# An adaLN block on one core: the setup phase dissolved into the first steps of the pipeline

## The chip, the cores and the metric

One core of a Trainium2 chip. The time is device microseconds of one execution, given as the median of several runs; lower is better. The profile is one further execution, recorded by the hardware profiler.

## The reference, cut to what matters

```python
x = L0_attn_x                                    # 8 batches, 512 tokens, 128 features, f32
mod = (_silu(L0_c) @ L0_wmod).reshape(8, 6, 1, -1)
sa, ca, ga, sb, cb, gb = (mod[:, i] for i in range(6))
ga = (2 * (ga >= 0) - 1) * jnp.maximum(jnp.abs(ga), 0.25)   # gb the same
h = _layernorm(x) * (1 + ca) + sa
x = x + ga * linear_attention(h)                 # 16 heads of 8, causal, elu features, projection, layer norm
h = _layernorm(x) * (1 + cb) + sb
x = x + gb * ffn(h)                              # layer norm, softmax attention, layer norm, mixture of 8 experts
```

Everything that depends on the conditioning vector c (the six rows of `mod` for each batch) is a small computation: SiLU of an 8 x 128 tensor, one product with 128 x 768 weights, signs and maxima of the gates.

## The kernel before

The kernel is three blocks in a row, each with its own instruction streams for the five engines, and a barrier of all engines between them: `setup_phase`, `attention` and `route` (the experts).

**Setup.** SP issues all loads on its one DMA queue (lines 208 to 215): c, the constants, the modulation weights, all of x in four loads of 512 KB, then the weights, those of the linear attention in twelve small loads (four of q and k, four bias columns, four of v). ACT computes the exponential of SiLU (L232), DVE the rest (L266 to L270), PE turns it (L241) and multiplies it with the modulation weights (L244 for shift and scale of the first norm, L247 for the other four rows). DVE works out the gates (L283 to L302), puts weights into another order of columns (L297, L305, L309), and copies the turned weights out (L317, L318). POOL fills the constant parts of the tiles `values` and `k_stack` (L225, L227). SP writes the modulation rows to memory, where they are read back broadcast to all partitions.

**Attention.** A software pipeline written out by hand: steps s from -3 to 8, each with eight slots d. In step s the engines work on stage a of batches s+3, s+2 and s+1, stage b (the causal linear attention, eight units g = 8s + d, one a slot) of batch s, and stage c of batches behind. Each engine has a list of `if d == ...` with what it does in a slot.
- Stage a: DVE takes statistics of x (`a_stats`, L1210 to L1217), POOL the reciprocal root (`a_rstd`, L643 to L647), ACT normalises (L1393), PE turns (`a_turn`, L877), ACT applies scale and shift of c (`a_h_out`, L1399), PE projects (`a_query` L882, `a_key` L887, `a_value` L892), ACT and DVE make features (exp L1404, ReLU L1234, sum L1239) and split them into three bf16 parts (ACT L1409, L1413; DVE L1245; POOL L651), which SP stores (L362, `linear_parts`).
- SP then reads the parts back in another arrangement into `q_stack` and `k_stack`, twelve loads (L380; for batch 0 in two halves of twelve). The stacks of two batches are kept in turn. PE multiplies them in `products` (L815), one unit ahead of the numerators: the first one of batch 1 stands in the last slot of step 0.
- DVE adds the output bias in `output` (L1206), the first of which waits for the seventeen late loads (L350), issued by SP at the start of the block: biases, gate and projection weights, gains, and `mod4` and `gb_all`, the broadcast modulation rows (2 MB and 512 KB). Before the first step, POOL clears the two tiles `spad` (L743); PE waits for both and DVE waits for both too.

## Time and profile before

| | us |
|---|---|
| median of 3 runs | 821.37 |
| lowest, highest | 821.14, 822.47 |
| the profiled execution's own time | 819.17 |
| its span | 817.4 |
| mean granted TensorE clock | 0.921 |
| PE busy | 656.6 (80%) |
| DVE busy | 601.7 (74%) |
| ACT busy | 495.7 (61%) |
| POOL busy | 435.2 (53%) |
| HBM read, written | 43.20 MB, 21.45 MB |

The span is the time from the first to the last recorded instruction; the execution's own time has 1.8 us more around it. Busy shares are means over phases that have different limits. The granted clock is TensorE's, as a share of its upper level of 2.4 GHz; 0.50 is the lower level, 1.2 GHz. Loads are recorded where they are issued (SPq); the transfer comes behind that.

### The profile page before, as it was taken

The page shows a single profiled execution, that of the slowest core. Times are in us where ns is not written, and L with a number is a line of the kernel's source. Part 1 is how long each engine was busy: PE and PEld are TensorE (multiplying, and loading weights), DVE is VectorE, ACT ScalarE, POOL GpSimd, SP SyncE. Part 2 cuts the span into 40 slices and gives each one's busy share as a digit, 9 for nine tenths or more (in the row PEclk, how much of TensorE's full clock was granted, in tenths as well). Part 3 has the DMA queues.
Part 4 walks back from the last instruction along what each step waited for, and adds up shares of the span by engine and source line. Part 5 has one row for each costly group of instructions (what it writes and reads, how often), then busy time and mean ns, then how long its engine had stood idle before and what let it go on. Part 6 is the DMA issues. An engine that isn't in the chain of part 4 may idle for free. (4 is left out here: it accounts for less than half of the span.)

```text
span 817.4 us, 16278 instructions
## 1 busy us (share of the span) xinstructions
PE 656.6 (80%) x5448; PEld 342.0 (42%) x5448; DVE 601.7 (74%) x1439; ACT 495.7 (61%) x1009; POOL 435.2 (53%) x953
## 2 busy tenths in 40 slices
PE   1338978899887797899999999999999734668784
PEld 0225656666655312223323333332332323567774
DVE  3445799998977998799999999999996154222332
ACT  0251456666545358788888888888888613233342
POOL 4220164765565433126666666666766734666653
PEclk9967999999999869999999999999999955988988
DMA  6334222533353211047212111121200012323210
GB/s 167 137 102 131 83 75 78 155 104 96 113 171 103 78 39 40 3 115 218 78 39 73 47 59 60 51 68 38 81 21 20 20 48 70 105 75 89 78 55 14
DMA packets 39409, 65.37 MB, mean 80 GB/s; under 512 B 6460, under 2 KB 32127, under 8 KB 36320
## 3 DMA queue, kind: packets, MB, share of 16 engines
q1 hardware_dynamic: 35584, 54.57, 21.8%
q0 software_dynamic: 3744, 9.77, 4.2%
q8 instruction: 45, 0.74, 0.4%
q14 instruction: 36, 0.29, 0.1%
HBM read 43.20 MB, written 21.45 MB: 79 GB/s over the span
## 5 line engine op out<-in xcount | busy, mean ns | idle before, releaser
L1457 ACT ACTIVATE arena<-pair 128x512 f32<-128x512 f32 x512 | 281.5, 602 | 51.7 <-PE pair L959 49.9
L1262 DVE TENSOR_REDUCE arena<-bank 128x1 f32<-128x512 f32 x388 | 250.6, 684 | 9.3 <-PE bank L938 8.4
L959 PE MATMUL pair<-q_stack,k_stack 49*128 49x512 bf16 x512 | 161.7, 387 | 8.0 <-ACT arena L1457 6.6
L938 PE MATMUL bank<-k_stack,q_stack 48*128 48x512 bf16 x388 | 137.5, 395 | 11.3 <-DVE arena L1262 4.8
L970 PE MATMUL bank<-arena,values 128*9 128x512 f32 x1024 | 135.6, 602 | 0.2 <-ACT arena L1457 0.2
L1181 DVE TENSOR_TENSOR arena<-bank,cst 128x512 f32<-128x512 f32 x128 | 82.2, 684 | 28.4 <-PE bank L815 27.9
L708 POOL TENSOR_TENSOR arena<-arena 128x1 f32<-128x1 f32 (+6 forms) x364 | 80.3, 221 | 28.5
L1262 DVE TENSOR_REDUCE arena<-pair 128x1 f32<-128x512 f32 x124 | 84.5, 681 | 1.7 <-PE pair L938 1.6
L938 PEld LDWEIGHTS bank<-k_stack,q_stack 48*128 48x128 bf16 x388 | 33.3, 93 | 110.6 <-issue 27.6
L959 PEld LDWEIGHTS pair<-q_stack,k_stack 49*128 49x128 bf16 x512 | 42.4, 93 | 60.1 <-ACT arena L1457 37.7
L1789 ACT ACTIVATE fq_all<-bank 128x512 f32<-128x512 f32 x39 | 23.2, 594 | 72.9 <-remote 37.8
L1377 ACT ACTIVATE arena<-bank,den_eps 128x512 f32<-128x512 f32 x32 | 21.7, 678 | 52.9 <-PE bank L841 52.9
L1869 PE MATMUL pair<-arena,fq_all 128*128 x208 | 32.7, 308 | 22.1 <-issue 12.5
L938 PE MATMUL pair<-k_stack,q_stack 48*128 48x512 bf16 x124 | 49.1, 396 | 1.2 <-DVE arena L1292 1.0
L1820 POOL DMA_INDIRECT out_dram<-arena,e_token_u x32 | 32.3, 1010 | 29.6 <-DVE arena L1697 22.8
L1860 PE MATMUL bank<-arena,h_all 128*128 128x128 f32 x312 | 47.8, 303 | 0.1
L1860 PEld LDWEIGHTS bank<-arena,h_all 128*128 128x128 f32 x312 | 44.8, 221 | 0.0
L830 PE MATMUL bank<-fq_all,arena 128*128 128x128 f32 x192 | 32.2, 292 | 14.0 <-ACT arena L1377 13.7
L656 POOL TENSOR_SCALAR arena<-arena 128x4 f32<-128x4 f32 x24 | 5.5, 229 | 70.7 <-DVE arena L1217 70.5
L1688 DVE TENSOR_SCALAR arena<-pair,lnw 128x128 f32<-128x128 f32 x39 | 15.9, 408 | 36.5 <-PE pair L1853 23.7
L841 PE MATMUL bank<-arena,values 128*9 128x128 f32 x1024 | 42.4, 286 | 0.0
L815 PE MATMUL bank<-q_stack,k_stack 48*128 48x128 bf16 x512 | 26.7, 227 | 17.9 <-DMA k_stack<-linear_parts 11.8
(261 smaller groups left out, 1269.5 us busy)
## 6 DMA issues: line engine op xcount, KB each, us to landing
linear_parts<-arena SPq DMA_DIRECT2D x8, 768.0 KB, 3.7
softmax_parts<-arena SPq DMA_DIRECT2D x8, 768.0 KB, 6.4
token_rows<-arena SPq DMA_DIRECT2D x32, 192.0 KB, 1.9
arena<-in_L_ffn_w_dram SPq DMA_DIRECT2D x16, 256.0 KB, 5.2
q_stack<-softmax_parts SPq DMA_DIRECT2D x16, 192.0 KB
k_stack<-softmax_parts SPq DMA_DIRECT2D x16, 192.0 KB
q_stack<-linear_parts SPq DMA_DIRECT2D x14, 192.0 KB
k_stack<-linear_parts SPq DMA_DIRECT2D x14, 192.0 KB
```

What stands on the lines that cost most here:

```text
L708: done(pool.tensor_tensor(half[:, 0:w], src[:, 0:w], src[:, w:2 * w], ALU.add))
L830: pe.matmul(b_nm[:, cols], spad[u][:, c - 1, cols], k.fq_all[:, b * L + c * P:b * L + (c + 1) * P], start=(gg == 0), stop=False, skip_grou ...
L841: last = pe.matmul(b_nm[VW * j:VW * j + E + 1, cols], vp[u][:, c, GH * (2 * hp + gg) + j, :], b_am[:, g % 2, gg, j, :], start=(c == 0), st ...
L938: pe.matmul(bank[:], qs[b % 2][rows, slot, qt * P:(qt + 1) * P], ks[b % 2][rows, slot, :], start=True, stop=True).then_inc(d_s_m, 1)
L959: pe.matmul(b_s[s % len(b_s)][:], ks[u][rows, 2 * g + x, kt * P:(kt + 1) * P], qs[u][rows, 2 * g + x, :], start=True, stop=True).then_inc( ...
L970: last = pe.matmul(b_num[VW * q:VW * q + E + 1, :], vp[b % 2][:, kt, GH * g + q, :], pt[:, kt % 2, q % 2, q // 2, :], start=(kt == 0), sto ...
L1181: dve.tensor_tensor(b_am[:, g % 2, gg], k.tiles(b_at[gg][:], GH), k.rep(k.causal, GH), ALU.mult).then_inc(s_am, 1)
L1262: dve.reduce_max(mx[:, m % 2, col:col + 1], bank[:], AX).then_inc(d_s_mr, 1)
L1457: act.activation(pt[:, kt % 2, x, half, :], b_s[s % len(b_s)][:], ACT.Exp, scale=SCALE).then_inc(d_s_e, 1)
L1820: pool.indirect_dma_start(out_rows, rows_at(token_u, j), yo[j], None, bounds_check=T * P - 1, oob_is_err=False).then_inc(s_sc, 16)
L1860: last = pe.matmul(b_up[j % R3][:, c * P:(c + 1) * P], w1c[j % R4][:, c * P:(c + 1) * P], xt[j % R4], start=True, stop=True)
L1869: last = pe.matmul(b_dn[j % R3][:, 0:D], hid[j % R4][:, c * P:(c + 1) * P], k.w2_all[:, bass.ds(e * HID + c * D, D)], start=(c == 0), stop ...
```

## The change

- `setup_phase` and its block, with the barrier behind it, are gone. Its buffers lie in the space of stage c, which is first used three steps later, and its semaphores are cleared at the end of the attention block.
- SP loads c, then batch 0 of x alone (256 KB), then the constants, the modulation weights, the v weights, batch 1 of x, the weights that are wanted later, and the rest of x. The eight loads of the q and k weights and biases are issued by ACT on its own queue, ahead of its exponential.
- `a_stats` waits for the load of its batch. DVE's small work stands in the slots: SiLU and all that the first projection wants (`silu`, `projection_weights`) in slot 3 of step -3, the gates and the weights in their new order (`modulations`) in slot 3 of step -2, the output weights in slot 7 of step -2. PE does its part ahead of its first step and in slots 2 and 5 of step -2 (the 512-column product stands in front of `a_query(0)`), ACT in slot 2 of step -2.
- POOL fills one `k_stack` and clears one `spad` in slot 3 of step -3, the other pair in slot 3 of step -2, each behind the `a_rstd` of that slot. SP waits for the fill of its `k_stack` before it loads batch 0's or batch 1's stacks.
- The seventeen late loads are issued behind batch 0's stack loads, with the two broadcasts last; POOL waits for them in step 1, no longer in step -1.

```diff
-        setup_phase(nc, k)
+        k.s_sc = top.enter_context(nc.semaphore("results_stored"))
         attention(nc, k)
         route(nc, k)
...
-def late_loads(nc, sp, k, sem):
+def late_loads(nc, sp, k, sem, stored):
...
     with nc.allow_non_contiguous_dma("columns of gains and shifts"):
-        for dst, src in loads:
+        for n, (dst, src) in enumerate(loads):
+            if n == len(loads) - 2:
+                sp.wait_ge(stored, 16)
             sp.dma_start(dst, src).then_inc(sem, 16)
...
-                sp.sem_clear(k.setup_semaphores)
-                late_loads(nc, sp, k, s_late)
+                sp.dma_start(c_raw, k.c_in).then_inc(w_s_c, 16)
+                x_in(0, 1, w_s_x[0])
+                sp.dma_start(k.cst[:], k.consts).then_inc(w_s_k, 16)
+                sp.dma_start(wm, k.wmod).then_inc(w_s_k, 16)
...
+                sp.wait_ge(w_s_mr, 5)
+                sp.dma_start(k.mod_dram.rearrange("i b d -> b i d"), mrow).then_inc(w_s_md, 16)
                 for s in STEPS:
...
                         wait(sp, s_at, NL * (a - 1))
+                        if a < 2:
+                            sp.wait_ge(w_s_f, 4 + a)
                         if a == 0:
                             for load in STACK_LOADS:
                                 load_stack(sp, k, k.linear_dram, 0, 0, *load, s_first, FIRST)
                             for load in STACK_LOADS:
                                 load_stack(sp, k, k.linear_dram, 0, 0, *load, k.s_stk[0], REST)
+                            late_loads(nc, sp, k, s_late, w_s_md)
...
-                for i in range(2):
-                    pool.memset(spad[i][:], 0.0).then_inc(s_pad, 1)
+                def filled(u):
+                    pool.memset(k.ks[u][:], 1.0).then_inc(w_s_f, 1)
+                    pool.memset(spad[u][:], 0.0).then_inc(s_pad, 1)
+
+                pool.memset(k.halfneg[:], -0.5).then_inc(w_s_f, 1)
+                for u in range(2):
+                    pool.memset(k.vp[u][:], 1.0).then_inc(w_s_f, 1)
+                pool.wait_ge(w_s_f, 1)
                 for s in STEPS:
-                    if s == -1:
+                    if s == 1:
                         pool.wait_ge(s_late, N_LATE)
...
                             if has(s + 3):
                                 a_rstd(s + 3)
+                            if s < -1:
+                                filled(s + 3)
...
+                        if s == -2 and d == 2:
+                            pe.matmul(k.bank[3][0:B, :], ct, wm[:, 2 * D:NM * D], start=True, stop=True
+                                      ).then_inc(w_s_m, 1)
...
                 def a_stats(a):
+                    dve.wait_ge(w_s_x[min(a, 2)], 16 if a < 2 else 16 * 3)
                     stats(k.x_all, a, a_st, a_mv, a_ve[:], a_s_st, a_s_mv, a_s_ve, a_s_nb)
...
-                dve.wait_ge(s_pad, 2)
...
+                        if s == -3 and d == 3:
+                            silu()
+                            projection_weights()
+                        if s == -2 and d == 3:
+                            modulations()
+                        if s == -2 and d == 7:
+                            output_weights()
...
                 def a_h_out(a):
                     act.wait_ge(a_s_tr, a + 1)
+                    if a == 0:
+                        act.wait_ge(w_s_v, PROJECT)
```

The order of the instructions on three engines at the places that matter. The names in square brackets are the semaphores waited for. First SP's queue, from batch 0's last stack loads to batch 1's, before (`linear_parts` is the store of a batch's parts):

```order
L380 DMA k_stack<-linear_parts 16x1x2048 x2
L380 DMA q_stack<-linear_parts 8x2048 x2
L380 DMA k_stack<-linear_parts 8x2048 x2
L362 DMA linear_parts<-arena 128x6x512 [waits a_part3]
L380 DMA q_stack<-linear_parts 24x1x4096 [waits a_parts_stored]
L380 DMA q_stack<-linear_parts 24x1x4096
```

and now:

```order
L207 DMA k_stack<-linear_parts 8x2048 x2
L177 DMA rows<-in_L_attn_bout_dram 128x128
L177 DMA gatew<-in_L_ffn_gate_w_dram 128x8
L177 DMA gateb<-in_L_ffn_gate_b_dram 128x8
L177 DMA lnw<-in_L_ffn_ln_w_dram 128x1
L177 DMA lnw<-in_L_ffn_ln_b_dram 128x1
L177 DMA lnw<-in_L_ffn_ln_w_dram 128x1
L177 DMA lnw<-in_L_ffn_ln_b_dram 128x1
L177 DMA wproj<-in_L_ffn_w_proj_dram 16x1x128 x8
L177 DMA arena<-modulation 128x4096 [waits modulation_stored]
L177 DMA gb_all<-modulation 128x1024
L189 DMA linear_parts<-arena 128x6x512 [waits a_part3]
```

The late loads, which stood at the head of the block before, now lie between the last stack load of batch 0 and the store of batch 1. Second, POOL from its fills to the second `a_rstd`, before:

```order
L227 MEMSET k_stack 128x4096 x2
L203 UNCONDITIONAL_BRANCH
L638 UNCONDITIONAL_BRANCH [waits barrier_Pool_Activation_PE_DVE_SP_gather]
L743 MEMSET arena 128x1536 x2
L643 ISA
L643 TENSOR_SCALAR arena<-arena 128x4 [waits a_variances]
L644 TENSOR_TENSOR arena<-arena,halfneg 128x4
L647 TENSOR_TENSOR arena<-arena 128x4 [waits a_rstd,a_mean_turned]
L643 TENSOR_SCALAR arena<-arena 128x4 [waits a_normed,a_variances]
L644 TENSOR_TENSOR arena<-arena,halfneg 128x4
L647 TENSOR_TENSOR arena<-arena 128x4 [waits a_rstd,a_mean_turned]
```

and now:

```order
L617 MEMSET values 128x576 x2
L512 ISA
L512 TENSOR_SCALAR arena<-arena 128x4 [waits a_variances,filled]
L513 TENSOR_TENSOR arena<-arena,halfneg 128x4
L516 TENSOR_TENSOR arena<-arena 128x4 [waits a_rstd,a_mean_turned]
L612 MEMSET k_stack 128x4096
L613 MEMSET arena 128x1536
L512 TENSOR_SCALAR arena<-arena 128x4 [waits a_normed,a_variances]
L513 TENSOR_TENSOR arena<-arena,halfneg 128x4
L516 TENSOR_TENSOR arena<-arena 128x4 [waits a_rstd,a_mean_turned]
L612 MEMSET k_stack 128x4096
L613 MEMSET arena 128x1536
```

The fills of the two `k_stack` were all ahead; now each stands with a clear of `spad` (the `arena` memset) behind an `a_rstd`, whose first instruction waits for `a_variances`. Third, DVE from the statistics of batch 1 to the features of batch 0, before:

```order
L1210 BN_STATS arena<-x_all 128x6 x4
L1213 MEMSET spare 128x1 [waits a_shift,a_stats]
L1215 BN_AGGR arena<-arena 128x2 x4
L1217 TENSOR_SCALAR arena<-arena 128x4 [waits a_means]
L1234 TENSOR_SCALAR fq_all<-pair,bq 128x512 [waits a_exp]
L1234 TENSOR_SCALAR arena<-pair,bq 128x512 [waits a_exp]
L1249 TENSOR_TENSOR v_all<-pair,rows 128x512 [waits a_v]
L1239 SCALAR_TENSOR_TENSOR fq_all<-arena,fq_all 128x512 [waits a_relu]
```

and now:

```order
L1141 COPY arena<-arena 128x2x32 [waits softmax_weights_in]
L1141 COPY arena<-arena 128x2x32
L1174 TENSOR_SCALAR arena<-arena 8x256 [waits vector_step]
L1176 TENSOR_TENSOR arena<-bank,arena 8x256 [waits vector_step]
L1178 TENSOR_SCALAR arena<-arena 8x256 [waits vector_step]
L1180 TENSOR_TENSOR arena<-arena 8x128 [waits vector_step]
L1181 TENSOR_TENSOR arena<-arena 8x128
L1183 TENSOR_TENSOR arena<-arena 8x128 [waits vector_step]
L1184 TENSOR_TENSOR arena<-arena 8x128
L1187 COPY wsm<-arena 128x8x8 x4
L1191 COPY wsm<-arena 128x4x16 x2
L1217 TENSOR_SCALAR fq_all<-pair,bq 128x512 [waits a_exp]
```

The gates, the modulation rows and the weights in new order (behind one more instruction on the gates, L1169) now stand between the statistics of batch 1 and the first ReLU of batch 0 (L1217, 1234 before).

## Rows read from the trace of the kernel before

**Rows 1.** The page: granted TensorE clock in the span's 40 slices.
```profile
PEclk9967999999999869999999999999999955988988
```

**Rows 2.** Timeline, 0.7 to 10 us: start, duration, engine, line, instruction, count, idle before.
```profile
0.74 1.28 ACT L232 ACT_TABLE_LOAD   x1 [0.74 <-PEq L1919]
...
1.81 6.96 POOL L227 MEMSET k_stack<- 128x4096 bf16 x2
...
5.65 0.31 ACT L232 ACTIVATE arena<-arena 8x128 f32<-8x128 f32 x1 [3.62 <-DMA arena<-in_L_wmod_dram]
5.99 2.85 DVE L266 TENSOR_SCALAR arena<-arena 8x128 f32<-8x128 f32 x1 [5.99 <-ACT arena L232]
...
8.88 0.94 DVE L268 RECIPROCAL arena<-arena 8x128 f32<-8x128 f32 x1
```

**Rows 3.** Timeline, 10 to 26 us: the rest of the setup phase.
```profile
10.69 0.76 SPq L215 DMA_DIRECT2D arena<-in_L_attn_Wqkv_dram  x1
...
11.67 1.88 PE L247 MATMUL bank<-arena 128*8 128x512 f32 x2
...
14.56 0.28 DVE L285 TENSOR_SCALAR arena<-arena 8x256 f32<-8x256 f32 x1
...
15.30 0.59 SPq L215 DMA_DIRECT2D bq<-in_L_attn_bqkv_dram  x1
...
20.05 0.90 PE L250 MATMUL bank<-cst,arena 128*128 128x128 f32 x3 [6.50 <-DMA arena<-in_L_attn_Wqkv_dram]
...
23.10 2.70 POOL L743 MEMSET arena<- 128x1536 f32 x2 [14.33 <-POOLq L203]
```

**Rows 4.** Timeline, 25 to 46 us: batch 0 through its first stages.
```profile
25.83 0.87 DVE L1210 BATCH_NORM_STATS2 arena<-x_all 128x6 f32<-128x128 f32 x4 [2.06 <-POOL arena L743]
...
29.09 1.65 ACT L1393 ACTIVATE arena<-x_all,arena 128x128 f32<-128x128 f32 x4 [15.08 <-POOL arena L647]
...
30.88 1.08 PE L877 MATMUL pair<-cst,arena 128*128 128x128 f32 x4 [9.71 <-ACT arena L1393]
...
32.83 2.08 PE L882 MATMUL pair<-arena,wlt 128*128 128x512 f32 x2 [0.87 <-ACT arena L1399]
...
35.66 0.75 DVE L1234 TENSOR_SCALAR fq_all<-pair,bq 128x512 f32<-128x512 f32 x1 [5.89 <-ACT arena L1404]
...
38.63 0.68 DVE L1239 SCALAR_TENSOR_TENSOR fq_all<-arena,fq_all 128x512 f32<-128x512 f32 x1
...
45.17 0.39 SPq L362 DMA_DIRECT2D linear_parts<-arena  x1
```

**Rows 5.** Timeline, SP's late loads: the first, modulation, gb_all, first lnw, wproj.
```profile
23.19 0.36 SPq L350 DMA_DIRECT2D rows<-in_L_attn_bout_dram  x1
...
24.54 0.43 SPq L350 DMA_DIRECT2D arena<-modulation  x1
...
27.68 5.16 SPq L350 DMA_DIRECT2D wproj<-in_L_ffn_w_proj_dram  x8
```

**Rows 6.** Windows: busy us (instructions) by engine, granted clock, DMA share, GB/s.
```profile
26.00:34.00 8.00, 2.26 (x6) 1.37 (x7) 2.57 (x20) 2.42 (x5) 2.91 (x6) 1.00 0.91 334
64.00:70.00 6.00, 5.16 (x56) 3.38 (x57) 3.24 (x8) 0.95 (x2) 0.00 (x0) 0.50 0.56 179
```

**Rows 7.** The page, part 6: stores of parts, KB, us to landing.
```profile
linear_parts<-arena SPq DMA_DIRECT2D x8, 768.0 KB, 3.7
softmax_parts<-arena SPq DMA_DIRECT2D x8, 768.0 KB, 6.4
```

**Rows 8.** Timeline, 62 to 88 us: batch 1's store, its first and last stack loads, their use.
```profile
62.96 0.39 SPq L362 DMA_DIRECT2D linear_parts<-arena  x1
...
66.73 1.36 SPq L380 DMA_DIRECT2D q_stack<-linear_parts  x2
...
73.60 0.63 SPq L380 DMA_DIRECT2D k_stack<-linear_parts  x2
...
87.76 0.40 PE L815 MATMUL bank<-q_stack,k_stack 48*128 48x128 bf16 x8
```

More of the change, by code:

```diff
@@ L431, in attention @@
         a_parts = a([6, L], BF16)
+        raw = carve(k.c_space)
+        wl_raw, wo_raw, wo_pos, bv_raw = raw([3, D]), raw([D]), raw([D]), raw([D])
+        ws_raw, wm, ct = raw([3 * D]), raw([NM * D]), raw([B])
+        c_raw, c_exp, c_rec, c_silu = (raw([D], parts=B) for i in range(4))
+        gamma_r, beta_r = raw([D], parts=B), raw([D], parts=B)
+        sgn, mag, mrow = raw([2, D], parts=B), raw([2, D], parts=B), raw([5, D], parts=B)
         spad = [b([C - 1, H * VW]) for i in range(2)]
@@ L1217, in stats, with done, after, silu @@
                     dve.tensor_scalar(ve, mv[:, :, 1], LN_EPS, None, ALU.add).then_inc(s_ve, 1)
+                step = [0]
+                def done(ins):
+                    step[0] += 1
+                    ins.then_inc(w_s_v, 1)
+                def after():
+                    dve.wait_ge(w_s_v, step[0])
+                def silu():
+                    dve.wait_ge(w_s_e, 1)
+                    done(dve.tensor_scalar(c_exp, c_exp, 1.0, None, ALU.add))
+                    after()
+                    done(dve.reciprocal(c_rec, c_exp))
+                    after()
+                    done(dve.tensor_tensor(c_silu, c_raw, c_rec, ALU.mult))
+                    assert step[0] == SILU
+                    dve.wait_ge(w_s_t, 1)
+                    done(dve.tensor_copy(ct, k.bank[1][:, 0:B]))
+                    assert step[0] == CT
@@ new lines, in positions, with projection_weights @@
+                def positions(dst, src, half):
+                    done(dve.tensor_copy(
+                        dst.rearrange("p (a h f) -> p a h f", a=2, h=2)[:, :, half, :].rearrange("p a (j e) -> p a j e", e=E),
+                        src.rearrange("p (a j h e) -> p a j h e", a=2, h=2, e=E)[:, :, :, half, :]))
+                def projection_weights():
+                    dve.wait_ge(w_s_t, 4)
+                    done(dve.tensor_copy(k.wlt[:], k.bank[0][:, 0:3 * P]))
+                    dve.wait_ge(w_s_l, 16 * 8)
+                    done(dve.tensor_scalar(k.bq2[:, 2:4], k.bq2[:, 0:2], FEAT_EPS, None, ALU.add))
+                    dve.wait_ge(w_s_b, 16 * 5)
+                    for half in range(2):
+                        positions(k.BV, bv_raw, half)
+                    dve.wait_ge(w_s_m, 1)
+                    done(dve.tensor_copy(k.sat[:], k.bank[2][:, 0:B]))
+                    done(dve.tensor_scalar(k.ca1t[:], k.bank[2][:, B:2 * B], 1.0, None, ALU.add))
+                    dve.wait_ge(w_s_k, 32)
+                    done(dve.reduce_sum(k.den_row[:], k.ident[:, E::VW], AX))
+                    after()
+                    done(dve.tensor_scalar(k.den_eps[:], k.den_row[:], FEAT_EPS * E ** 0.5, None, ALU.mult))
+                    after()
+                    assert step[0] == PROJECT
+                    dve.memset(b_nm[:], 0.0).then_inc(s_init, 1)
```

299 lines of the change are left out of this document (120 added, 179 removed).

## The prediction

> **What bounds the kernel now.** I read the clock slices of the page first, then the timeline from 0 to 100 us, then the windows. The clock is at its upper level nearly throughout, with a dip in the third and fourth slices [rows 1]. The phases behind 90 us are untouched and run from step to step with the engines busy, so what counts is when batch 0 and batch 1 enter them.
>
> Up to 23 us there is only the setup block: ACT waits until 5.65 us for the first three transfers, then a small chain over ACT, DVE and PE runs [rows 2, 3], and its end waits for weights. DVE's first look at x is at 25.83 us, since POOL clears two state tiles first (23.10 to 25.80) and DVE waited for them [rows 3, 4]. From there a chain runs through batch 0: statistics, normalise (29.09), transpose, projection (32.83), ReLU (35.66), features (38.63), store of the parts (45.17) [rows 4]. The stacks then come back from memory. Batch 1 follows: store at 62.96, its twelve stack loads issued from 66.73 to 74.23, used by PE at 87.76 [rows 8]. With 3.7 us for the last to land, as a store takes alone [rows 7], they are there at 77.9: PE is 9.9 us late for them, so batch 1 has 9.9 us to give.
>
> **The front, step by step**, in times of the new kernel.
> 1. x of batch 0 is the second transfer. In the kernel before, three transfers (756 KB) had landed at 5.65 [rows 2]; a 256 KB load issued at 1.2 lands between 3.2 and 5.6, I take 4.0. Statistics to normalised took 29.09 less 25.83 = 3.3 us [rows 4], so POOL has the shift at 7.2. Then it fills the first k_stack, 6.96/2 = 3.5 us [rows 2], to 10.7, and clears a state tile, 2.70/2 = 1.35 us [rows 3], to 12.05.
> 2. ACT issues eight loads before anything else. The same eight took SP from 10.69 to 15.89, 0.65 us each [rows 3]: ACT is free at 5.95, loads its table in 1.28, does the exponential in 0.31 [rows 2] and is done at 7.55. For the issue on ACT this trace has no row; I keep 0.65, between 0.3 and 1.3.
> 3. DVE's addition on that exponential is the doubtful one. It took 2.85 us for 128 elements [rows 2] where one of 256 elements takes 0.28 [rows 3], and it ended at 8.84, 0.07 us behind the second k_stack fill (8.77) [rows 2]. I read it as held until POOL's memset ended. Here the fill runs from 7.2 to 10.7 and the addition comes at 7.55, so it ends at 10.8. With the reciprocal (0.94) and a product (0.28) SiLU is there at 12.05.
> 4. PE: one transpose 0.3, three weight transposes 0.90 [rows 3], two products 1.0: 14.3. DVE's small work up to the count that releases the modulation of batch 0: 0.75, at 15.05. PE transposes batch 0 in 1.08 [rows 4] to 15.4, ACT modulates to 16.3. PE meanwhile does the 512-column product, 1.88 us [rows 3], now in front of the projection: this starts at 17.3 in place of 32.83 [rows 4], 15.5 us earlier.
> 5. DVE does the statistics of batch 1 to 17.1, POOL its rstd to 18.7 and then fills the second k_stack to 22.2. DVE's block of modulation work sits in front of the ReLU of batch 0. It waits for ACT's two rows (17.8), runs a step and two copies to 18.65, and then has a tensor_scalar from SBUF to SBUF, the kind of step 3, against the fill: held to 22.2. The rest, some 13 small instructions of 0.14 to 0.41, is 2.8 us: ReLU at 25.0, features at 26.9 in place of 38.63 [rows 4], **11.7 us earlier**. Undisturbed it would be 15.5.
>
> The page "SBUF — State Buffer", section "Who interferes with whom", in the Trainium skill, states such a lock: GpSimd and a VectorE operation in a two-port mode block each other for a whole instruction, copies and tensor_scalar included. By that rule step 3's row is as expected, and the weight copies in steps 4 and 5 are held behind the state clears too, up to 1.35 us more, which would make the time 818.7.
>
> The loads of the remaining x (1.5 MB) and of the output weights are issued by SP within the first 15 us and no one waits for them. The small copies of output weights (0.28 each) lie on DVE where ACT and PE have more to do. The removed barrier is inside the 11.7.
>
> **The late loads.** SP's 17 loads move from 23 us, where they were hidden, to a place between batch 0's last stack load and batch 1's store. In times of the kernel before: they take from 23.19 to 32.84 to issue, 9.65 us [rows 5], so the store goes from 62.96 to 72.6. The two broadcasts of the modulation (2.5 MB) are now last, the first issued at 71.7. In the kernel before they were issued at 24.54 [rows 5] and moved at 334 GB/s until about 33.3 (2.67 MB from 26 to 34 us) [rows 6]: 8.8 us, so they end at 80.5. The store is queued on the same rings. A store issued right behind twelve loads landed in 6.4 us and not 3.7 [rows 7], so it waits its turn; after 80.5 it needs about 2.6, landing at 83.1. Then the twelve loads, 77.9 less 66.73 = 11.2 us [rows 8]: 94.4. PE wants them at 87.76: **6.6 us of stall**. DVE's first output waits for the late loads too, at 80.6, about when they land; POOL's wait moves to step 1, when all is there. DVE and ACT have nothing that could be done in the stall beyond the step's own rest, so it stays.
>
> **The clock.** After the idle before batch 0's products PE ran at the lower level from 64 to 70 us (granted 0.50, 5.16 of 6 us busy) [rows 6]. The same follows the new stall. Between 0 (DVE hides it) and 2.2 us I take 1.1.
>
> **Sum:** -11.7 + 6.6 + 1.1 = -4.0 us. The profiled execution took 819.17 us (span 817.4), the median of the three runs is 2.2 above: 815.2 against 819.17, and **817.4 us** against 821.37. About 0.2% (1.6 us) can be told from no change.
>
> **Rivals.**
> - *The memsets do not hold DVE*, or DVE comes first. The races of steps 3 and 5 are decided by 0.35 and 0.05 us. Then features come 15.5 earlier: 813.4 us. Against it: the 2.85 us row. Chance 0.2.
> - *No stall for batch 1.* If the store passes the broadcasts, it lands at 76.3, the stacks at 87.5, just before 87.76: 821.4 - 11.7 = 809.7, and 806 with the first rival. For it: its margin of 9.9 us against 9.65 of issue. Against it: 6.4 against 3.7 in the page. Chance 0.15.
> - *Slower: the broadcasts are slow.* In the new place they share the memory with nothing, but their rate is one reading. If they move like the stack loads and stores of 64 to 70 us, 179 GB/s [rows 6], 2.67 MB takes 15 us and not 8: batch 1's store lands 7 later, DVE's first output waits as well, and the time is 817.4 + 7 = 824.4. It decides from a broadcast 4 us longer, some 220 GB/s. Against it: 334 GB/s with the same source and target. Chance 0.07.
> - *The front shrinks less*: ACT's issues at 1.3 us instead of 0.65, x0 late, the rest as above. Exponential at 12.8, no memset in its way then, SiLU at 14.3, 2.2 us later: 819.6. Chance 0.08.
>
> **How the numbers follow.** The forecast keeps 0.5, its own range 814 to 819.5 (broadcast and clock bounds). Faster by over 0.2% holds for the first two rivals, the forecast, and half of the last: 0.5 + 0.2 + 0.15 + 0.02 = 0.87. Within 0.2%: 0.06. Slower: 0.07. The range goes from 807.5 (most of the second rival) to 820.5, leaving out the slower case and a few per cent at the lower end.
>
> **What would show it.** The step that adds one to the exponential should last about 3 us and end with a k_stack fill; the first 512-wide ReLU at 25 us with a longish tensor_scalar shortly before; batch 0's store at 33.5; batch 1's store issued about 27.5 us behind it, landing some 10 us after issue; PE waiting for k_stack 6 to 7 us before the first product of batch 1, at the lower clock behind it. No wait there would refute the second term, a short addition and a ReLU near 21 the first. From batch 2 on everything should stand at one constant distance to the kernel before; if that distance drifts, the argument that nothing recovers is wrong.

## The result, and the profile after

The changed kernel takes **825.08 us** (median of 6 runs, 824.37 to 827.08) against 820.85 (6 runs, 819.47 to 822.47): the medians lie 0.52% apart, and the ratio over all runs is 1.0057, slower, with an interval of 1.0041 to 1.0072. I had forecast 817.4 with a range of 807.5 to 820.5. The profiled execution took 824.37 us (span 822.6) with a mean granted clock of 0.893, against 819.17, 817.4 and 0.921.

Of the page of the kernel after: the granted clock in the 40 slices [rows 1], the group of the products on `q_stack` (part 5: busy, mean ns, idle before, what ended most of it), and the stores of parts [rows 7].

```profile
PEclk9757799999999859999999999999999955798797
...
L692 PE MATMUL bank<-q_stack,k_stack 48*128 48x128 bf16 x512 | 27.8, 233 | 27.1 <-DMA k_stack<-linear_parts 22.1
...
linear_parts<-arena SPq DMA_DIRECT2D x8, 768.0 KB, 3.8
```

In its second to sixth slice the clock reads 7, 5, 7, 7, 9, where the kernel before had 9, 6, 7, 9, 9. This group now waits 22.1 us for `k_stack`, where it waited 11.8 in the kernel before. Nearly all of that difference is batch 1's 9.27 us, below.

**The front.** Timeline of the kernel after, 7 to 35 us, as in [rows 2 to 4] (start, duration, engine, line, instruction, count, idle before). `k_stack<-` and `arena<-` of POOL are the fill and the state clear, L1130 is the addition of SiLU, L1178 the maximum of the gates.

```profile
7.42 3.51 POOL L612 MEMSET k_stack<- 128x4096 bf16 x1
...
8.09 0.31 ACT L1518 ACTIVATE arena<-arena 8x128 f32<-8x128 f32 x1
...
8.43 3.89 DVE L1130 TENSOR_SCALAR arena<-arena 8x128 f32<-8x128 f32 x1 [2.75 <-ACT arena L1518]
...
10.87 1.38 POOL L613 MEMSET arena<- 128x1536 f32 x1
...
16.41 0.78 ACT L1393 ACTIVATE arena<-pair,sat,ca1t 128x512 f32<-128x512 f32 x1 [6.47 <-PE pair L754]
...
18.10 1.52 PE L761 MATMUL pair<-arena,wlt 128*128 128x512 f32 x2
...
19.67 3.51 POOL L612 MEMSET k_stack<- 128x4096 bf16 x1
...
20.15 4.49 DVE L1178 TENSOR_SCALAR arena<-arena 8x256 f32<-8x256 f32 x1
...
23.12 1.38 POOL L613 MEMSET arena<- 128x1536 f32 x1
...
26.21 0.73 DVE L1217 TENSOR_SCALAR fq_all<-pair,bq 128x512 f32<-128x512 f32 x1
...
28.13 0.67 DVE L1222 SCALAR_TENSOR_TENSOR fq_all<-arena,fq_all 128x512 f32<-128x512 f32 x1
...
34.65 0.36 SPq L189 DMA_DIRECT2D linear_parts<-arena  x1
```

The front comes out 10.5 us earlier: features at 28.13 in place of 38.63, batch 0's store at 34.65 in place of 45.17. Both doubtful steps were held, and longer than I had it: the addition ends at 12.32, behind the fill (10.93) and also behind the state clear (12.25), and the maximum at 24.64, behind the state clear that ends at 24.50.

**The late loads.** Timeline of the kernel after, 52 to 95 us, against [rows 5, 8].

```profile
52.55 0.37 SPq L177 DMA_DIRECT2D rows<-in_L_attn_bout_dram  x1
...
61.08 0.40 SPq L177 DMA_DIRECT2D arena<-modulation  x1
...
61.52 0.43 SPq L177 DMA_DIRECT2D gb_all<-modulation  x1
...
62.00 0.43 SPq L189 DMA_DIRECT2D linear_parts<-arena  x1
...
70.95 0.29 DVE L1106 TENSOR_TENSOR v_all<-pair,rows 128x128 f32<-128x128 f32 x1 [0.91 <-DMA gb_all<-modulation]
...
74.37 1.41 SPq L207 DMA_DIRECT2D q_stack<-linear_parts  x2
...
74.44 0.63 ACT L1403 ACTIVATE arena<-fq_all 128x512 bf16<-128x512 f32 x1 [2.44 <-DMA linear_parts<-arena]
...
87.64 0.61 PE L692 MATMUL bank<-q_stack,k_stack 48*128 48x128 bf16 x8 [9.27 <-DMA k_stack<-linear_parts]
...
91.09 0.61 PE L692 MATMUL bank<-q_stack,k_stack 48*128 48x128 bf16 x8
...
94.14 0.40 PE L692 MATMUL bank<-q_stack,k_stack 48*128 48x128 bf16 x8
```

Batch 1's first product stands at 87.64, in the kernel before at 87.76: the whole gain of the front is gone there. PE waited 9.27 us for it. The chain reads backward from that wait: the twelve stack loads were issued from 74.37, when the store had landed; the store was issued at 62.00, right behind the broadcasts, and took 12.4 us, not 3.7. DVE's first `output` (L1106) waited too, 0.91 us, until `gb_all` was there at 70.95, and so did ACT's first split of batch 2 (L1403), 2.44 us, until the store of batch 1 had landed. No run separates what this second wait costs.

**The clock.** Windows of the kernel after: busy us (instructions) by PE, PEld, DVE, ACT, POOL, granted clock, DMA share, GB/s.

```profile
62.00:70.00 8.00, 8.00 (x111) 5.63 (x111) 5.48 (x11) 2.01 (x4) 0.00 (x0) 1.00 0.98 326
80.00:86.00 6.00, 0.00 (x0) 0.00 (x0) 0.00 (x0) 0.00 (x0) 0.00 (x0) 0.50 0.50 157
86.00:94.00 8.00, 5.91 (x59) 3.71 (x59) 3.24 (x7) 1.89 (x4) 1.15 (x1) 0.50 0.16 54
```

PE stands still from 80 to 86 and then works at 0.50, the lower level of 1.2 GHz. The first products of the next two units follow after 3.45 and 3.05 us; in the kernel before they stood at 87.76, 90.13 and 91.91, so 2.37 and 1.78 us apart. Batch 2's store is at 91.92 against 91.42, batch 3's at 120.85 against 118.63, batch 4's at 147.27 against 144.68, and the last one of the softmax attention at 350.25 against 346.38. Against the kernel before, counted from batch 1's first product, 2.3 us are lost by batch 3's store, 2.7 by batch 4's, and 4.0 by the end of attention. The first two units alone make 2.35 of them (3.45 + 3.05 less 2.37 + 1.78).

### The profile page after: what moved, and what is told of

Read it like the earlier page. It is cut to its first block and busy times, and to the rows that moved or that the text cites. A ratio compares the mean times of both kernels' runs of the same rounds, so it can differ in the third digit from the quotient of the medians.

```text
span 822.6 us, 16273 instructions
## 1 busy us (share of the span) xinstructions
PE 661.9 (80%) x5448; PEld 347.3 (42%) x5448; DVE 607.8 (74%) x1439; ACT 495.8 (60%) x1009; POOL 433.7 (53%) x953
## 5 line engine op out<-in xcount | busy, mean ns | idle before, releaser
L817 PE MATMUL bank<-k_stack,q_stack 48*128 48x512 bf16 x388 | 138.0, 398 | 11.2 <-DVE arena L1245 5.0
L692 PE MATMUL bank<-q_stack,k_stack 48*128 48x128 bf16 x512 | 27.8, 233 | 27.1 <-DMA k_stack<-linear_parts 22.1
L1829 POOL DMA_INDIRECT out_dram<-arena,e_token_u x32 | 32.3, 1008 | 31.4 <-DVE arena L1706 22.1
L520 POOL TENSOR_TENSOR arena<-arena 128x512 bf16<-128x512 f32 x16 | 18.5, 1158 | 50.4 <-ACT arena L1407 50.4
L718 PE MATMUL bank<-arena,values 128*9 128x128 f32 x1024 | 44.6, 297 | 0.0
```

Of the source, the lines that this page charges most:

```text
L718: last = pe.matmul(b_nm[VW * j:VW * j + E + 1, cols], vp[u][:, c, GH * (2 * hp + gg) + j, :], b_am[:, g % 2, gg, j, :], start=(c == 0), st ...
L817: pe.matmul(bank[:], qs[b % 2][rows, slot, qt * P:(qt + 1) * P], ks[b % 2][rows, slot, :], start=True, stop=True).then_inc(d_s_m, 1)
L1829: pool.indirect_dma_start(out_rows, rows_at(token_u, j), yo[j], None, bounds_check=T * P - 1, oob_is_err=False).then_inc(s_sc, 16)
```

## The experiments

The twelve kernels ran in three jobs on three chips, on which the kernel before had medians of 818.05, 796.56 and 818.94 us. I therefore compare ratios to it, and medians within one job. The chips differ behind attention: in e7 (second job) the last softmax store stands at 349.0 us of a span of 797.5, in e11 (third job) the same kernel has it at 347.2 of 819.3. Positions in the first 100 us can be set beside each other between jobs to about 1 us: the changed kernel ran twice, for the result and as e9, with batch 0's store at 34.65 and 34.79 and batch 1's first product at 87.64 and 86.74. The theory: the late loads in front of batch 1's store take back what the front gains, by issue time and by bytes, and the lower clock behind the wait takes the rest; the memsets hold the front back by some 8 us. The rivals were that the slowness is the clock's alone, that it comes from the second queue, and that the front's gain has nowhere to go because something later bounds it.

### Is it the late loads?

**e1_late_early.** The small late loads go ahead of the store of the modulation rows, the broadcasts right behind it (part 0 are the fifteen small ones, part 1 the broadcasts).

```diff
+                late_loads(nc, sp, k, s_late, w_s_md, 0)
                 sp.wait_ge(w_s_mr, 5)
                 sp.dma_start(k.mod_dram.rearrange("i b d -> b i d"), mrow).then_inc(w_s_md, 16)
+                sp.wait_ge(w_s_md, 16)
+                late_loads(nc, sp, k, s_late, w_s_md, 1)
...
-                            late_loads(nc, sp, k, s_late, w_s_md)
```

> The changed kernel with its 17 late loads ahead of the pipeline again: the 15 small ones before the modulation rows are stored, the two broadcasts right behind that store. Theory (the front gained 10.5 us, and the late loads gave it back by holding batch 1's stacks): batch 1's first product comes at 78 to 80 us and no longer at 87.6, and the time is 811 to 814 us. Rival (the loss comes from the first steps themselves, from the lower clock or from the dissolved setup): that product still comes early, but the time stays at 820 or above, since later steps run slower in any case.

Measured: 806.5 us, ratio 0.9854 (0.9821 to 0.9888): the change becomes 1.5% faster than the kernel before. Timeline of e1, the second broadcast, batch 0's store, the first stack load of batch 0, batch 1's first product:

```profile
28.22 0.43 SPq L175 DMA_DIRECT2D gb_all<-modulation  x1
...
34.58 0.37 SPq L187 DMA_DIRECT2D linear_parts<-arena  x1
...
38.30 1.45 SPq L205 DMA_DIRECT2D q_stack<-linear_parts  x2
...
74.92 0.40 PE L692 MATMUL bank<-q_stack,k_stack 48*128 48x128 bf16 x8 [0.24 <-DVE arena L1081]
```

Batch 0's store lands in 3.7 us, since the broadcasts have 6.4 us to themselves in front of it (by the GB/s of one-microsecond windows I estimate that 2.4 of their 2.6 MB had moved when it was issued). Batch 1's product comes 12.7 us earlier than in the changed kernel and waits for DVE, not for `k_stack`. The granted clock is 1.00 from 70 to 90 us. The last softmax store stands 12.7 us ahead of the kernel before, so what the front gains does reach the end, and more than 10.5 of it. The other 2.2 us arise in two units of batch 0: the kernel before takes 4.93 us from the product at 67.40 to the next, e1 3.96 for the same unit, and 3.74 from 84.02 to batch 1's first product at a granted clock of 0.55, where e1 takes 2.48 at 1.00. No run shows that the clock is the whole reason. The rival that something later bounds the front's gain is out.

**e2_small_early.** Only the fifteen small ones go ahead; the broadcasts stay behind batch 0's stack loads. This splits issue time from bytes.

```diff
+                late_loads(nc, sp, k, s_late, w_s_md, 0)
                 sp.wait_ge(w_s_mr, 5)
...
-                            late_loads(nc, sp, k, s_late, w_s_md)
+                            sp.wait_ge(w_s_md, 16)
+                            late_loads(nc, sp, k, s_late, w_s_md, 1)
```

> Only the 15 small late loads go ahead; the two broadcasts (2.5 MB) stay between batch 0's stack loads and batch 1's store. If the bytes in front of the store count (the store queues behind them), the store is issued 8.5 us earlier but lands behind the broadcasts, about 12 us after its issue, batch 1's first product comes at 79 to 80.5 us with a short wait of 2 to 3 us, and the time is 815 to 818 us. If it was SP's issue time alone, the store lands 4 us after its issue and the time is 811 to 814, as with all of them early.

Measured: 811.02 us, ratio 0.9902 (0.9866 to 0.9937). Timeline of e2: batch 1's store, its first stack load, its first product.

```profile
53.45 0.43 SPq L187 DMA_DIRECT2D linear_parts<-arena  x1
...
64.58 1.37 SPq L205 DMA_DIRECT2D q_stack<-linear_parts  x2
...
78.48 0.40 PE L692 MATMUL bank<-q_stack,k_stack 48*128 48x128 bf16 x8 [2.71 <-DMA k_stack<-linear_parts]
```

The store is issued 8.5 us earlier than in the changed kernel (62.00), and still lands only after 11.1 us, behind 2.5 MB. Batch 1's product is 3.6 us later than in e1, where the bytes are out of the way, and 9.2 earlier than in the changed kernel. So both parts count, and the issue time of fifteen small loads counts most: 9.2 of the 12.7 us.

**e5_before_late_moved.** The reverse: the kernel before, with its setup phase, and nothing but the late loads moved behind batch 0's stack loads, broadcasts last.

```diff
                 sp.sem_clear(k.setup_semaphores)
-                late_loads(nc, sp, k, s_late)
...
                                 load_stack(sp, k, k.linear_dram, 0, 0, *load, k.s_stk[0], REST)
+                            late_loads(nc, sp, k, s_late)
...
-                    if s == -1:
+                    if s == 1:
                         pool.wait_ge(s_late, N_LATE)
```

> The kernel before, with the late loads alone moved to where the change has them (behind batch 0's stack loads, broadcasts last, POOL waiting for them in step 1). Theory: batch 1's first product 10 us later (98 us and not 87.8), some 2 us more at the lower clock behind it, 832 to 835 us in place of 821. My step before the run, 6.6 us of stall and 1.1 of clock, would give 828 to 829. Rival (the late loads are harmless by themselves, and cost only since the front is denser): below 825.

Measured: 833.17 us, ratio 1.016 (1.0122 to 1.0199). Timeline of e5: batch 1's store, its first stack load, its first product.

```profile
73.89 0.42 SPq L364 DMA_DIRECT2D linear_parts<-arena  x1
...
86.03 1.39 SPq L382 DMA_DIRECT2D q_stack<-linear_parts  x2
...
99.36 0.61 PE L817 MATMUL bank<-q_stack,k_stack 48*128 48x128 bf16 x8 [9.80 <-DMA k_stack<-linear_parts]
```

The product is 11.6 us later than in the kernel before. Of these, 1.6 were there already at batch 0's store (46.75 against 45.17; the setup phase ended later in this execution), which leaves 10.0 for the late loads: the size of the changed kernel's loss up to this place. From batch 3 to batch 4 the stores are 14.1 and 14.5 us late, so some 3 more come behind the wait, as in the changed kernel. This one edit costs more than the 10.5 us that the front gains.

### What holds the front

**e3_fills_moved.** Nothing but POOL's fills moves: the first pair ahead of the steps, the second from step -2 to step -1. DVE then waits for each state tile by itself.

```diff
+                filled(0)
                 pool.wait_ge(w_s_f, 1)
                 for s in STEPS:
...
-                            if s < -1:
-                                filled(s + 3)
+                            if s == -1:
+                                filled(1)
...
-                                if s == -1:
-                                    dve.wait_ge(s_pad, 2)
+                                if s < 1:
+                                    dve.wait_ge(s_pad, s + 2)
```

> The changed kernel with POOL's fills out of the way of DVE: the first k_stack and the first state tile before the first statistics are there, the second pair in slot 3 of step -1. Late loads as in the change. Theory (a memset on POOL holds a DVE tensor_scalar from SBUF to SBUF until it ends): the addition on SiLU's exponential falls from 3.89 to 0.2 to 0.3 us, the maximum of the gates from 4.49 to 0.3, batch 0's store goes from 34.65 to 27 us, and the time from 825 to 816 to 819. Rival (those two are long for another reason, code or the semaphore chain): they stay above 2 us and the time stays at 824 to 826.

Measured: 813.95 us, ratio 0.9961 (0.9935 to 0.9988). Timeline of e3: a small tensor_scalar of the statistics, the addition of SiLU, the maximum, batch 1's first product.

```profile
5.53 1.13 DVE L1118 TENSOR_SCALAR arena<-arena 128x4 f32<-128x4 f32 x1
...
8.41 0.22 DVE L1131 TENSOR_SCALAR arena<-arena 8x128 f32<-8x128 f32 x1 [1.75 <-ACT arena L1519]
...
16.20 0.28 DVE L1179 TENSOR_SCALAR arena<-arena 8x256 f32<-8x256 f32 x1
...
80.19 0.61 PE L693 MATMUL bank<-q_stack,k_stack 48*128 48x128 bf16 x8 [11.84 <-DMA k_stack<-linear_parts]
```

(The lines have moved by one: L1131 is the addition, L1179 the maximum.) The addition takes 0.22 us and not 3.89, the maximum 0.28 and not 4.49. Batch 0's store is at 26.50, 8.15 us earlier than in the changed kernel, and batch 1's product 7.45 earlier. The fills ahead of the steps have a price of their own: the state clear from 5.26 to 6.63 now holds a tensor_scalar of four columns, 1.13 us in place of 0.17. The wait of PE for `k_stack` stays (11.84 us here): the late loads are untouched.

**e4_both.** e3's fills, the small late loads ahead, and the two broadcasts behind batch 1's stack loads on a semaphore of their own, for which POOL waits in step 1.

```diff
-                            late_loads(nc, sp, k, s_late, w_s_md)
...
                                 load_stack(sp, k, k.linear_dram, a % 2, a, *load, k.s_stk[a % 2])
+                        if a == 1:
+                            sp.wait_ge(w_s_md, 16)
+                            late_loads(nc, sp, k, s_bc, w_s_md, 1)
...
                         pool.wait_ge(s_late, N_LATE)
+                        pool.wait_ge(s_bc, 32)
```

> Both repairs: fills as in the run with the fills moved, the 15 small late loads ahead, and the two broadcasts behind batch 1's stack loads, on a semaphore of their own that only POOL waits for in step 1. Theory: nothing gives the front's gain back; batch 0's store at 26.5 us as in the run with the fills moved, batch 1's first product at 67 to 68 us (72.4 in the run with the late loads early, less 8, plus one unit), 20 us earlier than in the kernel before, ratio to before 0.975 to 0.978. Rival (a limit behind the front, such as SP's queue or batch 1's stacks, comes up once the front is this short): batch 1's product at 70 or later, ratio above 0.98.

Measured: 775.72 us, ratio **0.9741** (0.9715 to 0.9767), the best version of all and 2.6% faster than the kernel before. Timeline of e4: batch 1's store, the first broadcast, batch 1's first product.

```profile
44.60 0.39 SPq L187 DMA_DIRECT2D linear_parts<-arena  x1
...
55.54 0.35 SPq L175 DMA_DIRECT2D arena<-modulation  x1
...
67.78 0.40 PE L696 MATMUL bank<-q_stack,k_stack 48*128 48x128 bf16 x8 [0.24 <-DVE arena L1085]
```

The store lands in 3.9 us, the broadcasts follow behind the stack loads, and the product stands 20.0 us ahead of the kernel before, waiting for DVE alone.

**e8_fills_moved_late_early.** The same fills with e1's place for the broadcasts, right behind the store of the modulation rows (the two diffs of e1 and e3 together).

> Fills moved and all 17 late loads ahead of the pipeline, the two broadcasts right behind the store of the modulation rows, thus right in front of batch 0's store. Theory (a store queues behind the broadcasts): batch 0's store is issued at 26.5 but lands 1 to 4 us later than the usual 3.7, the first product of batch 0 comes at 41 to 43 us against 38.5 with the broadcasts elsewhere, ratio to before 0.978 to 0.983, 2 to 4 us above the run with both repairs. Rival (the broadcasts are done by then): no difference to the run with both repairs.

Measured: 781.98 us, ratio 0.9825 (0.9798 to 0.9851), 0.8% above e4 in the same job. Timeline of e8: second broadcast, batch 0's store, its first stack load.

```profile
24.83 0.43 SPq L175 DMA_DIRECT2D gb_all<-modulation  x1
...
26.83 0.37 SPq L187 DMA_DIRECT2D linear_parts<-arena  x1
...
36.11 1.46 SPq L205 DMA_DIRECT2D q_stack<-linear_parts  x2
```

With the fills gone, batch 0's store comes 2.0 us behind the broadcasts and not 6.4 as in e1, and it lands after 9.3 us. I had expected 1 to 4 us over 3.7 and it was 5.6. Batch 0's first product came at 45.09, not at 41 to 43. What was a free place for the broadcasts in e1 is not one here. Batch 1's product stands at 72.89 against 67.78 in e4.

### What the lower clock costs

**e6_pe_kept_busy** and **e10_pe_kept_busy_longer.** PE does 30 or 42 products of 128 x 128 that nobody reads before the first unit of batch 1, so that it does not stand still in the wait. The trace shows two records for each, 60 and 84.

```diff
+                    if g == NL:
+                        pe.wait_ge(s_am, 2 * g)
+                        for i in range(30):
+                            pe.matmul(b_at[i % 2][:, 0:P], k.wlt[:, 0:P], k.wlt[:, P:2 * P], start=True, stop=True)
                     if g == 0:
                         pe.wait_ge(s_first, N_STACK)
```

> The changed kernel, with 30 products that nobody reads (128 x 128 x 128, f32, from constant weights into the banks of the next products) in front of PE's wait for batch 1's stacks, so that PE is busy through most of that wait. Theory (2 to 3 us behind the wait are lost because PE works at the lower clock there): granted clock 1.0 from 80 to 100 us, the first two units of batch 1 take 2.4 and 1.8 us as in the kernel before and not 3.5 and 3.1, and the time is 2 to 3 us below the changed kernel, 822 to 823. Rival (the units are slow because DVE, ACT or the banks have a backlog): the same spacing as in the change, same time or more.

Measured: 799.02 us, ratio 1.0034 (1.0014 to 1.0054). The products ran from 76.12 to 83.94, PE then waited another 2.99 us, the clock was 0.53 from 88 to 95, and the units followed after 2.83 and 3.09 us. The edit didn't do what it was for, so it says nothing on the price of the clock. Its front shows something else. Timeline of e6, the second pair of memsets and the maximum:

```profile
20.10 3.51 POOL L612 MEMSET k_stack<- 128x4096 bf16 x1
...
20.59 3.16 DVE L1182 TENSOR_SCALAR arena<-arena 8x256 f32<-8x256 f32 x1
23.55 1.52 POOL L613 MEMSET arena<- 128x1536 f32 x1
```

Here the maximum ended at 23.75, 0.14 us behind the fill, and the state clear that came next took 1.52 us in place of 1.38. In e6's first pair, and in both pairs of the changed kernel and of e9, the DVE instruction ended only behind the second memset.

**e9_change_again** is the changed kernel once more, as a neighbour for e10 on the same chip.

> The changed kernel as it is, beside the next three on one chip, since chips differ by some per cent in the last phase. Expected: ratio to before 1.004 to 1.007, as at first; the three others are read against this one.

Measured: 823.64 us, ratio 1.0066 (1.0045 to 1.0088), which agrees with the first measurement. The addition took 4.03 us and the maximum 4.49, batch 1's product was at 86.74, the units 3.46 and 3.09 apart.

> As the run with PE kept busy, but with 42 unread products: the 30 took 7.8 us and ended at 84, 3 us ahead of the stacks, and the clock fell again at 89. 42 should end within 1 us of the stacks. Theory (the 2 to 3 us behind the wait are the lower clock's): granted clock 1.0 up to 96 us at least, the first two units of batch 1 take 2.4 and 1.8 us, batch 2's store is issued 3 us earlier than in the change as counted from batch 1's first product, ratio 0.002 to 0.003 below that of the change on this chip. Rival (the lower clock only moves to another place and costs the same there): the two units are short, but the later stores stand no earlier than in the change, same ratio.

Measured: 820.8 us, ratio 1.0022 (1.0001 to 1.0043). Windows of e9 and then of e10, columns as above:

```profile
88.00:95.00 7.00, 6.55 (x68) 3.92 (x61) 3.69 (x9) 1.95 (x5) 1.16 (x1) 0.50 0.35 116
110.00:116.00 6.00, 6.00 (x44) 4.72 (x46) 5.68 (x10) 3.91 (x9) 3.70 (x3) 0.50 0.01 3
```

```profile
88.00:95.00 7.00, 5.52 (x93) 3.85 (x92) 4.40 (x10) 2.68 (x7) 1.16 (x1) 1.00 0.20 67
110.00:116.00 6.00, 3.94 (x66) 2.81 (x64) 5.97 (x12) 4.58 (x11) 2.63 (x2) 1.00 0.00 0
```

With the products running until 88.17 the clock stays at 1.00, the upper level, and the units follow after 2.37 and 1.79 us as in the kernel before. Batch 1's product is 2.3 us later than in e9 (89.04, the products stand in its way), and yet batch 3's store is 2.2 us earlier (119.91 against 122.06) and the last one of the softmax attention 2.7 (347.64 against 350.34). Counted from batch 1's first product that is 4.5 us up to batch 3's store and 5.0 up to the last: the price of the lower clock on this chip, where e9 has a second stretch at 0.50 from 110 to 116 us. Up to batch 2's store, the place named in the expectation, it is only 0.6 and not 3. In the change's first profile, counted the same way against the kernel before, it was 2.3 up to batch 3's store and 4.0 up to the last. The medians lie 2.8 us apart, since e10 starts 2.3 later; the intervals of the two ratios miss each other by 0.0002 only, so the sign is shown and the size rests on the stores. The slowness is not the clock's alone: e10 has none of it and is no faster than the kernel before.

### Is it the second queue?

**e7_one_queue**, **e11_one_queue_again** (the same kernel, beside e9) and **e12_both_one_queue** (the same edit on e4). ACT's eight loads are issued by SP, behind the v weights.

```diff
-                            act.dma_start(wl_raw[64 * half:64 * half + 64, z, :], rows_of[half]).then_inc(w_s_l, 16)
-                            act.dma_start(k.bq2[64 * half:64 * half + 64, z:z + 1], bias_of[half]).then_inc(w_s_l, 16)
+                            sp.dma_start(wl_raw[64 * half:64 * half + 64, z, :], rows_of[half]).then_inc(w_s_l, 16)
+                            sp.dma_start(k.bq2[64 * half:64 * half + 64, z:z + 1], bias_of[half]).then_inc(w_s_l, 16)
```

> The changed kernel with the eight loads of the q and k weights issued by SP again, ahead of batch 1's x; everything else as in the change. ACT is then free from the start: exponential at 3.5 to 4 us, the addition on DVE at 6 us, ahead of POOL's fill, SiLU at 7.5 us in place of 13.6. The weights land at 13 us, and PE's transposes wait for them, about when SiLU was there in the change. Theory (the second queue only trades one wait for another here): modulation of batch 0 at 15.5 to 16.5 us, as in the change (16.4), time within 1 us of the change. Rival (the second queue carries part of the front's gain): modulation at 18 or later and the time 2 us above the change.

Measured: 798.01 us, ratio 1.0018 (0.9999 to 1.0037). The modulation came at 15.09 and batch 0's store at 33.29, 1.4 us earlier than in the change. The ratio is 0.0039 below that of the change (1.0057, another chip), some 3 us where the theory had at most 1, and not above it, as the rival had it.

> The changed kernel with the eight loads of ACT on SP's queue, again, now beside the change. Its first run had the modulation of batch 0 at 15.09 us against 16.41 in the change, and a ratio of 1.0018. Theory (with the fills where the change has them, ACT's eight issues ahead of its exponential cost more than SP's queue gains): batch 0's store 1.3 us earlier than in the change, ratio 0.001 to 0.004 below it. Rival: no difference.

Measured: 820.88 us, ratio 1.0027 (1.0008 to 1.0047), against 1.0066 for the change in the same job. Timeline of e11: the addition of SiLU, and PE's three weight transposes.

```profile
5.44 0.21 DVE L1137 TENSOR_SCALAR arena<-arena 8x128 f32<-8x128 f32 x1
...
12.60 0.90 PE L1004 MATMUL bank<-cst,arena 128*128 128x128 f32 x3 [5.34 <-DMA bq<-in_L_attn_bqkv_dram]
```

With one queue ACT's exponential is done at 2.5 us and the addition comes at 5.44, ahead of POOL's fill: it takes 0.21 us. Then PE waits for the weights, until 12.60. The modulation of batch 0 still comes at 15.14 in place of 16.54, and batch 0's store at 33.38 in place of 34.79. So up to batch 0's store the second queue makes the change 1.4 us slower, not faster: it delays the exponential into the memset. The medians point the same way (820.88 against 823.64), with intervals that overlap.

> Both repairs, and the eight loads on SP's queue. Here SiLU is no longer held, so PE waits for the weights: they land at about 13 us, modulation of batch 0 at 15 us against 12.7 with two queues. Theory (the second queue pays once POOL's fills are out of the way): batch 0's store at 28.5 to 29.5 us against 26.65, ratio 0.977 to 0.978 against 0.974. Rival (something else ends the front): the same ratio as with two queues.

Measured: 801.94 us, ratio 0.9798 (0.9769 to 0.9827), against 0.9741 for e4 in another job. The modulation comes at 15.12 and not 12.73, batch 0's store at 29.16 and not 26.65. With the fills out of the way the second queue is worth 2.4 us at the modulation. The slowness of the change is not the queue's in either case.

## Why the prediction was wrong

It had the sign wrong. Its sum was -11.7 + 6.6 + 1.1; up to the end of attention the trace shows -10.5 + 10.4 + 4.0.

- **Steps 1 and 2 were right in kind**: x of batch 0 was there at 4.18 (4.0), POOL's fill began at 7.42 (7.2). ACT's eight issues took 6.05 us and not 5.2, 0.6 of that in the first, which took 1.25 us; so the exponential ended at 8.40 and not 7.55.
- **Steps 3 and 5, right in kind, undersized.** "I read it as held until POOL's memset ended" is confirmed by e3 (3.89 to 0.22 us, 4.49 to 0.28). But I ended the hold with the fill, and it lasted through the state clear right behind it, 1.4 us more each time. The modulation came at 16.41 (15.5), the projection at 18.10 (17.3), the ReLU at 26.21 (25.0), the front 10.5 us earlier and not 11.7. The rule of the Trainium skill, page "SBUF — State Buffer", section "Who interferes with whom", agrees as far as it goes: a VectorE operation in a two-port mode, which tensor_scalar can enter, and a GpSimd instruction exclude each other, and the one that comes first holds the shared ports for its whole instruction. By it I had looked for holds of the weight copies in steps 4 and 5; those were not held, since POOL was idle by then. Whether the waiting VectorE instruction is served between two GpSimd memsets in a row stands outside the sentence I used. It was not in the changed kernel, and it was once in e6.
- **The late loads, the step that failed first**: "6.6 us of stall" was 10.4. The mechanism was right, and two terms of it were too small. Issue of the seventeen loads was 9.45 us (9.65) and the store's place 62.00, as the sum has it with the front's 1.2 us less. The two terms behind it were short. Broadcasts and store took 12.4 us from the store's issue and not 10.5: the broadcasts were there at 70.95, 9.9 us from their issue and not 8.8, and the store came 3.4 later and not 2.6. The twelve loads took 13.3 us up to PE's first use, where I had 11.2. That 11.2 rested on "with 3.7 us for the last to land", a store's figure put on a load. The windows of the kernel before show that it was wrong there already (columns as above):

```profile
77.00:78.00 1.00, 1.00 (x12) 1.00 (x11) 0.30 (x1) 1.00 (x4) 0.00 (x0) 1.00 0.28 57
78.00:79.00 1.00, 1.00 (x22) 0.73 (x23) 0.82 (x2) 0.61 (x2) 0.00 (x0) 1.00 0.11 33
79.00:80.00 1.00, 1.00 (x21) 0.78 (x14) 1.00 (x2) 0.00 (x0) 0.00 (x0) 1.00 0.00 0
```

Its own stack loads moved bytes until 79, 4.8 us after the last issue at 74.23. In the kernel after, the last bytes moved by 86.5 (windows of 0.25 us) and PE's product came 1.1 us later at 87.64. With the same 1.1 us the margin of the kernel before was some 7.7 us and not 9.9, an estimate from these rows. This row was there to be read.
- **The clock, the other term that failed: 1.1 was 4.0** for all that is lost behind batch 1's first product. I had bounded it at 2.2, from one idle stretch ahead of batch 0; the first two units behind the wait alone took 2.35 longer. e10 keeps PE at work in the wait, and the distances from batch 1's first product are then those of the kernel before (258.6 us to the last softmax store in both, 262.6 in the kernel after). Beside e9, its neighbour, e10 puts the price at 4.5 to 5.0; in the first profile the 1.7 us behind batch 3's store have no run of their own.
- **The rivals.** "No stall for batch 1" fell: the store did not pass the broadcasts. e2 and e8 show the same with 11.1 and 9.3 us. For this the Trainium skill, page "DMA: Bandwidth & Descriptors", section "Queues, rings and completion order", has that each DMA engine takes the descriptors of a ring in order; the trace agrees, with 3.7 us where nearly all of the broadcasts had moved (e1) and 9.3 to 12.4 where, by the same kind of estimate as for e1, 2 MB or more of them still stood in front. The slower side was given 0.07, on one mechanism, broadcasts at half their rate. They moved at 326 GB/s (334 before). The time came out there by three terms a little short each (1.2 in the front, 1.9 and 2.1 in the loads) and one further short (2.9 behind batch 1's first product). Less the 0.2 us by which the issue of the loads was shorter, these are 7.9 us, from the forecast -4.0 to the +3.9 at the end of attention; the medians are 4.2 apart and the two profiled executions 5.2. The upper end of my range, 820.5, let only one of them go wrong at a time.
- **"DVE and ACT have nothing that could be done in the stall"** held, in so far as PE, DVE and ACT all show 0.00 us of work from 80 to 86 us. The test "From batch 2 on everything should stand at one constant distance to the kernel before" came out otherwise: it drifts from +0.5 at batch 2's store to +2.2 at batch 3's and +3.9 at the end of attention. But that is a loss growing, not a recovery. The first part is the lower clock, as e10 shows, whose stores from batch 2 to batch 7 stand at one distance of +1.3. Between batch 4's store and the end of attention another 1.3 us come in, 0.35 of them by batch 5's store and 0.9 behind batch 7's; that was not tried, and stays open.

## What to carry to other kernels

A load that is off the path has to be costed at its new place by three numbers: its issue time on the queue, its bytes in front of the next transfer on the same queue, and what a late transfer then does to PE's clock. Where VectorE works on SBUF against long GpSimd memsets, count to the end of the last memset of the run (every hold that met the first of two memsets in these runs ended there, but for one in e6), and put such fills where VectorE has nothing to do. A margin is read from the last bytes that move and the first use, not from the last issue plus another transfer's latency, and terms that all err to one side must be added up in the range.

## What the runs showed of the hardware

- A VectorE tensor_scalar (8 x 128 or 8 x 256, 0.21 to 0.28 us alone) that met a POOL memset took 3.89, 4.03 and 4.49 us. It ended 0.07 to 0.14 us behind the second of two memsets that followed each other without a gap, not behind the first. Once, in e6, it ended 0.14 us behind the first, after 3.16 us, and the second memset took 1.52 us in place of 1.38.
- A 768 KB store that lands in 3.7 us alone took 12.4, 11.1 and 12.3 us (the change, e2, e3) issued 0.5 us behind 2.5 MB of broadcasts on its queue, and 9.3 us issued 2.0 us behind them (e8).
- A DMA issue on ACT's queue took 0.60 to 0.73 us, the first one 1.25, against 0.59 to 0.65 for the same loads on SP (e11).
- After 9.3 us without a product, PE ran its next two units at 1.2 GHz, 3.45 and 3.05 us long and not 2.37 and 1.78. With products that nobody read in the gap, up to 0.9 us before the first unit, it ran them at 2.4 GHz (e10). Where those products ended 3.0 us before the first unit, the granted clock was 0.53 from 88 to 95 us (e6).
